# Adaptive attention block on one core: matmuls cut into column tiles, a new order of steps, row sums of long chunks over one added tile, and up-projection weights built transposed

## The reference

```
# 1. adapter whose weights are modulated by the condition
w_down = down_project * (cond @ down_gamma) + (cond @ down_beta)      # (256, 64)
w_up   = up_project   * (cond @ up_gamma)   + (cond @ up_beta)        # (64, 256)
h      = relu(x @ w_down) @ w_up + x
# 2. attention over soft tree paths, 8 heads of 32, depth 5, causal
paths  = sigmoid(h @ Wp + bp);  V = h @ Wv
agree  = pq*pk + (1-pq)*(1-pk);  sim = cumprod(agree).sum() / 5
x      = x + softmax(causal(sim)) @ V @ Wo
# 3. low-rank weight from the condition, then one of 8 experts for each token
U      = (cond @ W_dec + b_dec).reshape(257, 30);  z = x @ (U[:256] @ V2) + U[256] @ V2
x      = x + z + expert_w[argmax(z @ gate_w.T)] @ z
```

## Time and profile before

| | |
|---|---|
| runs, median (lowest to highest) | 170.01 us (169.91 to 173.27), 3 runs |
| profiled execution, device time | 169.74 us |
| its span, first to last instruction | 167.3 us |
| TensorE matmul busy | 149.8 us, 90% |
| VectorE, ScalarE, GpSimd busy | 45%, 35%, 17% |
| chain that ended last | TensorE 76%, VectorE 12%, DMA 4%, ScalarE 3% |
| mean granted TensorE clock | 0.990 |

### The profile page before, as it was taken

The page is one execution under the profiler, slowest core; times in us unless marked ns, Lnnn a source line. Parts: engine busy times, 40 slices in busy tenths (PEclk is TensorE's granted clock), DMA queues, the critical chain, the costliest instruction groups (busy, mean ns, idle before and its releaser), DMA issues.

```text
span 167.3 us, 3934 instructions
## 1 busy us (share of the span) xinstructions
PE 149.8 (90%) x1728; PEld 102.3 (61%) x1728; DVE 75.3 (45%) x148; ACT 58.9 (35%) x70; POOL 29.1 (17%) x56
## 2 busy tenths in 40 slices
PE   6989489999965899987999899968999999999893
PEld 6656255654733577555676577646776766667672
DVE  0570708086705854177026365086143754164341
ACT  3004353725730424554430334466223447301010
POOL 8000022003022100250220200250222025200000
PEclk9999999999999999997899999999999999999999
DMA  5999999000220000000000010000011000010111
GB/s 127 295 427 449 387 365 289 16 4 0 33 31 4 0 4 0 4 0 0 4 33 31 31 35 0 4 0 4 11 52 35 31 4 0 4 63 31 63 34 64
DMA packets 7376, 12.42 MB, mean 74 GB/s; under 512 B 1552, under 2 KB 5808, under 8 KB 7232
## 3 DMA queue, kind: packets, MB, share of 16 engines
q10 hardware_dynamic: 2496, 7.23, 11.1%
q1 hardware_dynamic: 4768, 4.89, 9.2%
q0 software_dynamic: 96, 0.05, 0.8%
HBM read 9.95 MB, written 2.22 MB: 73 GB/s over the span
## 4 chain that ended last, share of the span: by engine, by line
PE 76%; DVE 12%; DMA 4%; ACT 3%; issue 2%; SPq 1%; POOL 0%; POOLq 0%; DVEq 0%; ACTq 0%
PE work L539 35%; PE c_ps L539 21%; PE s_ps L539 15%; DVE feat L530 4%; DMA u_scratch<-u_row 2%; PE work L700 2%; DVE h_t L439 2%; DMA u_raw<-u_scratch 2%; PE work L640 1%; DVE rden L404 1%; ACT prob L349 1%; DVE u_w L473 1%; ACT phi_t L374 1%; DVE x_t L519 1%; SPq L285 1%
## 5 line engine op out<-in xcount | busy, mean ns | idle before, releaser
L349 ACT ACTIVATE prob<-s_ps 128x1536 f32<-128x1536 f32 (+1 forms) x24 | 38.2, 1591 | 36.1 <-PE s_ps L539 35.9
L404 DVE RECIPROCAL rden<-c_ps 128x256 f32<-128x256 f32 x16 | 28.1, 1757 | 20.0 <-PE c_ps L539 20.0
L328 POOL TENSOR_SCALAR_AFFINE_SELECT prob<-prob 128x1024 f32<-128x1024 f32 x16 | 18.1, 1132 | 107.1 <-ACT prob L349 107.1
L539 PE MATMUL c_ps<-prob,v_sb 128*32 128x256 f32 (+1 forms) x384 | 26.8, 351 | 0.0
L539 PE MATMUL s_ps<-phi_t 32*128 32x256 f32 (+1 forms) x384 | 24.9, 374 | 1.5 <-ACT phi_t L374 1.0
L539 PE MATMUL c_ps<-prob,ones 128*32 128x256 f32 (+1 forms) x384 | 26.1, 344 | 0.0
L539 PEld LDWEIGHTS s_ps<-phi_t 32*128 32x128 f32 x384 | 17.9, 190 | 9.3 <-issue 5.4
L519 DVE TENSOR_TENSOR x_t<-work,x_t 128x256 f32<-128x256 f32 x16 | 6.8, 423 | 29.3 <-PE work L539 29.3
L539 PE MATMUL work<-ctx_t,mix_sb 128*128 128x256 f32 x64 | 17.8, 401 | 1.2 <-DVE h_t L439 0.8
L539 PEld LDWEIGHTS c_ps<-prob,v_sb 128*32 128x32 f32 x384 | 10.3, 110 | 11.0 <-issue 4.3
L539 PE MATMUL work<-zo_t,gexp 128*128 128x256 f32 x64 | 16.5, 381 | 0.0
(11 more groups left out here) (92 smaller groups left out, 120.1 us busy)
## 6 DMA issues: line engine op xcount, KB each, us to landing
wdec<-in_W_dec ACTq DMA_DIRECT2D x1, 3855.0 KB, 14.8
x_t<-in_x_tr SPq DMA_DIRECT2D x4, 512.0 KB, 9.2
ex_t<-in_expert_tr ACTq DMA_DIRECT2D x1, 2048.0 KB, 23.0
out_x<-x_t SPq DMA_DIRECT2D x16, 128.0 KB, 1.7
mix_sb<-in_mix ACTq DMA_DIRECT2D x1, 776.0 KB, 16.5
lift_sb<-in_lift ACTq DMA_DIRECT2D x1, 384.0 KB, 4.3
w_vl<-in_vl SPq DMA_DIRECT2D x1, 296.0 KB, 5.5
first_sb<-in_first SPq DMA_DIRECT2D x1, 144.0 KB, 4.0
```

Of the source, the lines that this page charges most:

```text
L328: nc.gpsimd.affine_select(out=tri, in_=tri, compare_op=ALU.is_ge, fill=0.0, base=0, pattern=[[0, HG], [0, 2], [1, P]], channel_multiplier= ...
L349: nc.scalar.activation(prob[:, p % 2, :, 0:width(p)], s_ps[:, :, 0:width(p)], ACT.Exp).then_inc(exped, 1)
L404: link(nc.vector.reciprocal(rden[:], c_ps[m % 2][:, CW:2 * CW]))
L539: return nc.tensor.matmul(o, w, r, start=start, stop=stop, skip_group_check=True)
```

## The change

Five things change.

- **Column tiles.** A helper `tiled` issues a 128x128 matmul as four of 128x32 with the same moving operand, each into its 32 partitions of the output. `VL`, `WoU` and `out` use it; `down` uses four tiles of 32 in place of two of 64.
- **Row sums of a long chunk.** The first pair of a long chunk no longer has the eight matmuls of ones. A new VectorE step, `add`, adds its two units (each 4 heads x 256) into `tiles`, and the context of the last pair starts with four matmuls of ones over `tiles`. ScalarE's exponential two pairs on waits for the add too.
- **Up-projection weights.** A step `ugT` makes gamma and beta as columns (four matmuls with 4 moving columns); VectorE builds the weights transposed, 8 `tensor_scalar` of 128x128 with two scalars for each partition, and signals `lift_ready`; `gup` is now two transposes and one VectorE copy of 128x256.
- **Order.** `phi` of the next batch moves from after context 3 (of six, counted from 0) to after scores 5. `zT` comes one or two gaps earlier, `zs` and `zo` follow in the next gap, both `zoT` stand together, `out` stands next to a `context`. `Uadd` goes behind `G 1`, `Q` and `WoU` move.
- The opening and the banks of the opening are set to fit.

```
 PROLOGUE = [
-("gdn", (0,)), ("gup", 0), ("down", 0), ("gup", 1), ...
+("gdn", (0,)), ("ugT",), ("down", 0), ("gup", 0), ("gup", 1), ...

 def after_scores(b):
     gaps[0] += [("up", n1, 0), ("up", n1, 1)]
+    gaps[4] += [("phi", n1, 0), ("phi", n1, 1)]
     if b == 0:
...
-        gaps[4] += [("Q",), ("Uadd",)]
-        gaps[5] += [("G", 1)]
+        gaps[5] += [("G", 1), ("Uadd",)]
     elif n1 < B:
-        gaps[1] += [("VL", n1, 0), ("VL", n1, 1)]
+        gaps[1] += [("zs", prv, ALL_T), ("zo", prv, 0), ("zo", prv, 1), ("VL", n1, 0), ("VL", n1, 1)]
...
-    if b == 1:
-        gaps[0] += [("WoU",)]
-    if prv >= 1:
-        gaps[0] += [("out", prv - 1, 3)]
+    else:
+        gaps[1] += [("zs", prv, ALL_T), ("zo", prv, 0), ("zo", prv, 1)]
+        gaps[4] += [("zs", b, FIRST), ("zo", b, 0)]
     if prv >= 0:
-        gaps[4] += [("zoT", prv, 1)]
-        gaps[5] += [("out", prv, 1)]
+        gaps[3] += [("zoT", prv, 0), ("zoT", prv, 1)]

 def after_context(b):
     if b == 0:
...
-        gaps[4] += [("ubT",), ("G", 0)]
-    if prv >= 0:
-        gaps[1] += [("zT", prv, ALL_T)]
-        gaps[2] += [("zs", prv, ALL_T), ("zo", prv, 0), ("zo", prv, 1)]
-        gaps[3] += [("zoT", prv, 0)]
-        gaps[4] += [("out", prv, 0)]
+        gaps[3] += [("Q",)]
+        gaps[4] += [("G", 0), ("ubT",)]
+        gaps[5] += [("down", n2), ("WoU",)]
+    else:
+        gaps[0] += [("zT", prv, ALL_T)]
+        gaps[3] += [("out", prv, 0)]
+        gaps[4] += [("out", prv, 1)]
         gaps[5] += [("out", prv, 2)]
-    if n1 < B:
-        gaps[3] += [("phi", n1, 0), ("phi", n1, 1)]
+    if prv >= 1:
+        gaps[1] += [("out", prv - 1, 3)]
...
         ORDER += _c
+        if _p + 1 < ALL and opening(_p + 1):
+            ORDER += [("add", _p + 1)]
-ORDER += [("out", B - 1, 0), ("zT", B - 1, SECOND), ("zs", B - 1, SECOND), ...
+ORDER += [("zT", B - 1, SECOND), ("out", B - 1, 0), ("zs", B - 1, SECOND), ...

 # ScalarE, the exponential
                     if p >= 2:
                         act.wait_ge(summed, p - 1)
+                        if opening(p - 2):
+                            act.wait_ge(added, adds(p - 2))
 # VectorE
+                elif kind == "ugT":
+                    full(dve, s)
+                    nc.vector.tensor_copy(ug_col..., bank(s)[:, 0:2 * DC * B]).then_inc(empty(s), 1)
+                    done(dve, s)
+                    for b in range(B):
+                        for c in range(DC):
+                            ins = nc.vector.tensor_scalar(w_lift[:, b, c, :], uproj_t[:, c, :], ug_col[:, c, b:b + 1],
+                                                          ug_col[:, DC + c, b:b + 1], op0=ALU.mult, op1=ALU.add)
+                        ins.then_inc(lift_ready, 1)
                 elif kind == "gup":
-                    link(nc.vector.tensor_tensor(w_up[:, b, :], uproj[:], bank(s)[:, 0:D], ALU.mult))
-                    nc.vector.tensor_tensor(w_up[:, b, :], w_up[:, b, :], bank(s)[:, D:2 * D], ALU.add
-                                            ).then_inc(empty(s), 1)
+                    nc.vector.tensor_copy(w_up[:, s[1], :], bank(s)[:, 0:D]).then_inc(empty(s), 1)
+                elif kind == "add":
+                    p = s[1]
+                    both = prob[:, p % 2].rearrange("p h (s q) -> p h s q", s=2)
+                    dve.wait_ge(exped, p + 1)
+                    nc.vector.tensor_tensor(tiles[:, chunk(p) % 2], both[:, :, 0, :], both[:, :, 1, :], ALU.add
+                                            ).then_inc(added, 1)
 # TensorE
+            def tiled(o, w, r, start, stop):
+                for j in range(P // DH):
+                    part = slice(DH * j, DH * (j + 1))
+                    ins = mm(o[part], w[:, part], r, start=start, stop=stop)
+                return ins
...  (in context)
+                if half and last:
+                    pe.wait_ge(added, adds(p))
+                    for h in range(HG):
+                        mm(c_ps[m % 2][DH * h:DH * (h + 1), CW:2 * CW], ones[:], tiles[:, m % 2, h, :],
+                           start=False, stop=False)
...
+                    if half and first:
+                        continue
+                elif kind == "ugT":
+                    for g in range(2 * DC):
+                        ins = mm(o[:, B * g:B * (g + 1)], gam_up[:, P * g:P * (g + 1)], cond_c[:, 0:B])
                 elif kind == "gup":
-                    ins = mm(o[:], cond_b[:, s[1], :], gam_up[:])
+                    pe.wait_ge(lift_ready, s[1] + 1)
+                    for c in range(DC):
+                        ins = nc.tensor.transpose(o[:, P * c:P * (c + 1)], w_lift[:, s[1], c, :], ident[:])
```

More of the change, by code:

```diff
@@ L61, in masks, with opening, adds @@
     return sum(pair(i)[1][3] for i in range(p + 1))
+def opening(p):
+    return pair(p)[1][1] == 1 and pair(p)[1][4]
+def adds(p):
+    return sum(opening(i) for i in range(p + 1))
 ALL_T, FIRST, SECOND = (0, 1, 2, 3), (0, 1), (2, 3)
-PROLOGUE = [("gdn", (0,)), ("gup", 0), ("down", 0), ("gup", 1), ("up", 0, 0), ("up", 0, 1), ("gdn", (1, 2, 3)),
+PROLOGUE = [("gdn", (0,)), ("ugT",), ("down", 0), ("gup", 0), ("gup", 1), ("up", 0, 0), ("up", 0, 1), ("gdn", (1, 2, 3)),
             ("VL", 0, 0), ("VL", 0, 1), ("VL", 0, 2), ("VL", 0, 3), ("bias", 0), ("tanh", 0), ("feat", 0),
             ("gup", 2), ("gup", 3), ("phi", 0, 0), ("phi", 0, 1), ("scores", 0), ("down", 1)]
-EARLY_BANK = {("gdn", (0,)): 0, ("gup", 0): 1, ("down", 0): 2, ("gup", 1): 3, ("up", 0, 0): 4, ("up", 0, 1): 5,
-              ("gdn", (1, 2, 3)): 0, ("VL", 0, 0): 1, ("VL", 0, 1): 2, ("VL", 0, 2): 3, ("VL", 0, 3): 4,
-              ("gup", 2): 0, ("gup", 3): 1, ("phi", 0, 0): 5, ("phi", 0, 1): 2}
+EARLY_BANK = {("gdn", (0,)): 0, ("ugT",): 1, ("gup", 0): 0, ("down", 0): 2, ("gup", 1): 3, ("up", 0, 0): 4, ("up", 0, 1): 5,
+              ("gdn", (1, 2, 3)): 1, ("VL", 0, 0): 0, ("VL", 0, 1): 2, ("VL", 0, 2): 3, ("VL", 0, 3): 4,
+              ("gup", 2): 1, ("gup", 3): 0, ("phi", 0, 0): 5, ("phi", 0, 1): 2}
 def after_scores(b):
@@ L114, in after_context @@
         gaps[2] += [("bias", n1), ("tanh", n1), ("feat", n1)]
-    if n1 < B:
-        gaps[3] += [("phi", n1, 0), ("phi", n1, 1)]
-    if n2 < B:
+    if prv >= 1:
+        gaps[1] += [("out", prv - 1, 3)]
+    if b >= 1 and n2 < B:
         gaps[5] += [("down", n2)]
@@ L120, in after_context @@
         gaps[2] += [("zT", b, FIRST)]
-        gaps[4] += [("zs", b, FIRST), ("zo", b, 0)]
-        gaps[5] += [("zoT", b, 0), ("out", prv, 3)]
+        gaps[5] = [("zoT", b, 0), ("out", prv, 2), ("out", prv, 3)]
     return gaps
@@ L133 @@
         ORDER += _c
-ORDER += [("out", B - 1, 0), ("zT", B - 1, SECOND), ("zs", B - 1, SECOND), ("zo", B - 1, 1),
+        if _p + 1 < ALL and opening(_p + 1):
+            ORDER += [("add", _p + 1)]
+ORDER += [("zT", B - 1, SECOND), ("out", B - 1, 0), ("zs", B - 1, SECOND), ("zo", B - 1, 1),
           ("out", B - 1, 1), ("zoT", B - 1, 1), ("out", B - 1, 2), ("out", B - 1, 3)]
-NO_BANK = ("scores", "context", "bias", "tanh", "feat", "Uadd", "zo")
+NO_BANK = ("scores", "context", "add", "bias", "tanh", "feat", "Uadd", "zo")
 EARLY = 6
@@ L188, in build @@
         w_dn = sb("w_dn", [P, B, DC, HD])
+        ug_col = sb("ug_col", [P, 2 * DC, B])
+        w_lift = sb("w_lift", [P, B, DC, P])
         w_up = sb("w_up", [P, B, D])
@@ L196, in build @@
         q_bd = sb("q_bd", [P, TT, E])
+        tiles = sb("tiles", [P, 2, HG, CW])
         gexp = sb("gexp", [P, 2, D])
@@ L235, in build @@
         consts = sem("consts")
+        lift_ready = sem("lift_ready")
         wide_ready = sem("wide_ready")
@@ L246, in build @@
         summed = sem("summed")
+        added = sem("added")
         ctx_ready = sem("ctx_ready")
@@ L427, in _ @@
                     ins.then_inc(empty(s), 1)
+                elif kind == "ugT":
+                    full(dve, s)
+                    nc.vector.tensor_copy(ug_col[:].rearrange("p g b -> p (g b)"), bank(s)[:, 0:2 * DC * B]
+                                          ).then_inc(empty(s), 1)
+                    done(dve, s)
[4 more added lines that the diff above has]
+                        ins.then_inc(lift_ready, 1)
                 elif kind == "gup":
[L429 to L430 removed]
                     full(dve, s)
[L432 to L434 removed]
+                    nc.vector.tensor_copy(w_up[:, s[1], :], bank(s)[:, 0:D]).then_inc(empty(s), 1)
                 elif kind == "up":
@@ L613, in _ @@
                     for c in range(DC):
-                        for j in range(2):
-                            ins = mm(o[HD * j:HD * (j + 1), 0:T // 2], w_dn[:, b, c, :],
-                                     x_t[:, b, c, T // 2 * j:T // 2 * (j + 1)], start=(c == 0), stop=(c == DC - 1))
+                        for j in range(4):
+                            ins = mm(o[DH * j:DH * (j + 1), 0:T // 2], w_dn[:, b, c, DH * (j % 2):DH * (j % 2 + 1)],
+                                     x_t[:, b, c, T // 2 * (j // 2):T // 2 * (j // 2 + 1)],
```

(13 more changed lines are left out.)

6 lines of the change are left out of this document (3 added, 3 removed).

## The result

The changed kernel takes 159.11 us in the median (157.44 to 160.69, 4 runs) against 171.64 (169.91 to 173.29, 4 runs) of the kernel before. The ratio of comparable runs is 0.9268, 95% interval 0.9229 to 0.9308: 7.3% faster. The forecast was 156.5 us, 153.5 to 160.5. The profiled execution took 157.61 us against 169.74 before, with two low-clock stretches against one; the sum of the forecast is meant for it. Its terms add up to 156.24 (it rounds to 156.3), which is 1.4 short.

A forecast was written before the change was run, and what follows sets the result against it. TensorE, holding 76% of the chain of waits, was taken to bound the kernel. 169.74 - 3.5 - 3.4 + 0.3 - 5.9 - 1.0 = 156.3 us, with the median put at 156.5, range 153.5 to 160.5.

The forecast's parts named there:

- Row sums, -3.5: Long chunks: eight groups of ones of 0.434 us leave TensorE, saving 3.5 us; add costs nothing here outside batch 0.
- Changes of shape, -3.4: TensorE's list: 14 fewer entries into 128-wide tiles, 4 fewer for `down`, 2 more into narrow tiles, saving 3.4 us.
- The unpriced assumption: In `out`, four tiles reading the same moving operand stream like a context's four different ones; no row showed it.
- Opening, +0.3: Before the first `up`: copies and eight `tensor_scalar` on VectorE move its start from 8.85 to 9.1; bounds -0.1 and +0.7.
- Waits, -5.9: TensorE's waits after the opening: 11.3 us today, 5.4 left or new, so 5.9 saved; bounds 3.5 and 7.
- Clock, -1.0: Low stretch at 77.0 to 80.5 goes, saving 1.7 us; one in the opening costs 0.7; bounds -1.7 and +1.
- The granted clock falls under 0.97: One of the signs in the profile after that would show the forecast wrong.
- The restless clock: Rival: three more low-clock stretches in lulls of batch 0 and the opening, 161.6 us; chance 0.07.
- VectorE did not become the bound: Rival: VectorE becomes the bound and all adds land on the path, 166.4 us; chance 0.08.
- issue: Rival: narrow matmuls held up by their issue, 0.248 us a pass over 192 passes, 162.7 us; chance 0.03.
- open weight loads: Rival: weight loads of `out` and `VL` not hidden, 0.44 us a pass, about 199 us; chance 0.04.

The follow-up runs named there:

- e_oldgup: The changed kernel with the up-projection weights made as before (no `ugT`, VectorE's multiply and add as before): 156.07 us.
- e_late: e_oldgup with the features of batch 1 moved on VectorE behind the copies of `U 1` and `U 2`: 153.40 us, ratio 0.907.
- e_late_noadd: e_late without the adds, matmuls of ones again in both pairs of a long chunk: 156.39 us.
- e_order: The kernel before with only the new order of steps; no column tiles, no adds, old up-projection weights: 160.15 us, ratio 0.950.
- e_order_tiles: The kernel before with the new order and the column tiles; no adds, old up-projection weights: 156.78 us.
- e_after: The changed kernel run once more with no edit, as base for later runs: 158.78 us.
- e_tiles: The kernel before with only the column tiles, in the old order: 166.06 us, ratio 0.985.
- e_fill: The changed kernel with 10 idle matmuls in the lull before the first `phi` and 3 before `scores 0`: 157.11 us.

## Why the prediction was right, step by step

**Row sums, -3.5.** The stream was right; the add takes 1.21 us, taken as 1.24. The cost of the add was put at nothing except in batch 0, and that one cost, 2.2 us at `U 3`, is what ate most of the gain: 0.7 us was left by the medians (1.0 from `up` on), 3.0 come back when it is out of the way (e_oldgup, e_late, e_late_noadd). In the forecast that cost stood under the waits, so the sum wasn't hurt, but its reader would overrate the step.

**Changes of shape, -3.4.** 3.37 between e_order and e_order_tiles, where 3.0 follows from their own lists; by the same count the order alone saves another 0.5 of such changes. The unpriced assumption, one moving operand for four tiles, holds: 0.86 for four passes.

**Opening, +0.3.** Mis-sized. `up` started at 9.68, not 9.1 (8.85 before). The eight `tensor_scalar` of the changed kernel, as one group:

```profile
7.16 2.14 DVE L454 TENSOR_SCALAR w_lift<-lift_sb,ug_col 128x128 f32<-128x128 f32 x8
```

They lie 0.27 us apart where 0.17 was taken and 0.23 was the upper bound. The forecast reckoned that one source is quicker than two, by the copy in rows 8; with two scalars for each partition it was slower than the two-source operation (0.336 us each against 0.283). That makes +0.83, 0.5 us more than forecast and just outside the bound of +0.7. A little of it is the start of the execution: e_after and e_late, whose first `gdn` runs at the same slow pace, have `up` at 10.11 and 9.40, 0.7 apart.

**Waits, -5.9.** Right in which waits go and which come. `ub_col`, `feat` and the later `h_t` are gone; `U 3` was put at 2.0 and is 2.2 printed, `Q` at 1.1 and is 1.0. e_order shows that the waits were the largest part, as the sum had it: 9.9 us for the order, of which the sum gives 1.7 to the low stretch that went with them. The size is less sure. Four waits of 3.7 us printed are left behind the opening; by the forecast's own reckoning (0.17 more for each) that is 4.4, where it left 5.4, so 6.9 would be saved. The traces give 5.7: 12.6 from `up` on, less 3.5, 3.3 for the tiles and 0.1 for the clock. That the term came out within 0.2 is partly luck, and an exact split of the 9.9 wasn't measured.

**Clock, -1.0.** The place was right, the size not: two stretches came where one was reckoned, and 1.7 us where 0.7 stood. From `up` on the traces differ by 158.4 - 145.8 = 12.6 us, where these steps say 3.5 + 3.4 + 5.9 + 1.0 = 13.8; the clock is 1.0 of the 1.2 that are missing. With 0.5 from the opening, and 0.3 given back because the change leaves 2.1 us around the span and not 2.4, that is the miss of 1.4. The experiments give the same 12.6: 9.9 for the order, 3.3 for the tiles, 1.0 for the adds, less 1.6 for the low clock that the new weights bring (145.8 - 144.2). "The granted clock falls under 0.97" was named as a sign that the forecast is wrong; in half the runs it did, 0.968, and these are the runs at 159.8 to 160.7, above the forecast, and two of them, 160.60 and 160.69, above the range. The median of four, 159.11, lies in the range because two of its runs had only two low stretches; with a third at 0.968 it would have come to about the upper end, 160.5. The range held partly by luck.

**Rivals.** The restless clock came in part. It asked for three more stretches, in the opening and in lulls of batch 0, and 161.6 us; half of the eight runs of the changed kernel had three stretches against one before, and took 159.8 to 160.7. The one seen in a trace outside the opening lies in batch 0, behind `U 3`. The argument against it, that the 3.1 us wait for `ub_col` brought no fall, is true of that trace but was no ground to build on: in e_tiles a low stretch starts right behind a wait of 2.1 for it. VectorE did not become the bound (54% busy), but in batch 0 its queue did set the path, which is the small form of that rival. Narrow matmuls cost neither issue nor open weight loads: e_tiles would have shown either by itself.

## What to carry to other kernels

Write TensorE's time as stream, changes of tile shape and waits: each had a price in the trace of before, and the parts added up (9.9 for the order, 3.3 for the tiles, 1.0 for the adds from `up` on, measured one on the other). Compare traces from a step behind the opening, or a start at half pace can pass for a gain. Work moved off the bounding engine is paid in the queue it goes to: look at what stands behind the new instruction there before counting it as free, and move it, not only add it. And a step that lightens an engine in a lull can make its clock fall; here the lighter `gup` did so, and idle matmuls or the old, heavier weights prevented it in the opening.

## What the runs showed of the hardware that was not expected

- The kernel before is spread by its clock. Over the 22 runs beside the experiments, 5 at mean clock 1.0 took 167.85 to 168.82 us, 9 at 0.99 168.30 to 170.09, 6 at 0.98 170.97 to 171.95, and one each at 0.97 and 0.96 173.38 and 174.73: the medians of the first three levels are 168.75, 168.78 and 171.08. So the first stretch costs nothing that these runs show, the second 2.3 us, and the four together about 6 (167.85 to 168.82 against 174.73). The half pace of the start is mixed into these times. Each kernel with the new order and the old up-projection weights ran within 1.4 us.
- A transpose group slows with the clock like a matmul group: 1.94 us against 1.07 in the opening.
- Of a VectorE add of 128x1024 and a GpSimd mask of 128x1024 that meet, the second to start takes 2.12 us: the add instead of 1.21, or the mask instead of 1.10.
- The granted clock in the profile reads 1.00 from the first instruction on, but the first 18 passes of 128 columns in the kernel before lie 0.22 us apart (1.59 to 5.59 us), and eight such passes of `phi` in e_fill take 0.91 us, 0.11 each. The end of that pace is what moves `up` between 8.31 and 9.86 us in four kernels with one opening.
